# A transformer layer on eight cores: per-tile LayerNorm statistics and whole-tile query chains in place of pairs and halves

## The chip, the cores and the metric

The kernel runs on the 8 cores of one Trainium2 chip, the same program on each, every core on its own two sequences of 2048 tokens. The cores don't talk to each other. The metric is the device time of the slowest core in microseconds.

## What is computed

x is 16 x 2048 x 1024 in fp32. It is normalised once (LayerNorm without weights), and from the result two branches are computed and added to x: linear attention with 16 heads of 64, and a feed-forward part whose 8 binary trees of depth 7 mask the activations.

```python
xn = (x - mean) / sqrt(var + 1e-5)
q, k, v = (split_heads(xn @ W.T + b) for W, b in ((Wq,bq), (Wk,bk), (Wv,bv)))
q, k = feature_map(q), feature_map(k)          # where(x > 0, x + 1, exp(x))
kv = einsum('bhnd,bhnm->bhdm', k, v);  k_sum = k.sum(axis=2)
attn = (q @ kv / maximum(q . k_sum, 1e-6)) @ Wo.T + bo
logits = xn @ W_in.T + b_in                    # 8 trees x 255 nodes = 2040
acts = silu(logits);  dmap = nodes on the path that (logits > 0) takes, per tree
y = x + attn + (acts * dmap) @ W_out.T
```

## The kernel before

A core has 32 tiles of 128 tokens, 16 for each of its two sequences. Weights stay in SBUF as bf16. The code is written by hand, instruction by instruction, each engine with its own queue in program order; `em.wait` makes an engine wait for a semaphore value and `em.sig` raises one. Two loops run over the tiles, since the attention needs the sums over all tokens of a sequence first.

**Pass 1** (L336 on) computes K and V of a tile and adds to the sums `p_kv` and `p_ksb` of its sequence. TensorE's order in iteration t is: K matmuls of t (L344), the sums of tile t-1 (L309 to L319), the 8 transposes of the normalised tile t+1 (`emit_xnt`, L265), the V matmuls of t (L370, L378). K goes through ScalarE (copies at L352 and L356, the copy of the transposed tile at L271, Relu at L389, Exp at L392), V is copied by the vector engine (L396, L399), which also makes `s_phik` (L404). The LayerNorm statistics come in two parts: `emit_sums` takes the row sum on the vector engine (L200) and the sum of squares on ScalarE (L195), and `emit_pair` turns the sums of two tiles into mean and reciprocal root with 21 instructions on 128 x 2 numbers, each waiting for the one ahead (a reciprocal and four Newton steps). `emit_xnstt` (L253) then writes each normalised tile `s_xn`. Pairs are emitted at the end of even iterations, for tiles t+2 and t+3. There are four x buffers and two of `s_xn`. The statistics are kept in `s_stats` for pass 2.

**Pass 2** (L635 on) reloads x, normalises it with the stored statistics (`emit_ln`, L182), and computes query, trees and output. TensorE's order in iteration t is: Wq matmuls of t+1 (L462, L464), first half of the logits of t+1 (L479), the transposes of `s_qp` of t in two groups of four (L654, L659), the attention products in two groups of eight heads (L674, L683), the transposes of the masked activations (L698, L700), the Wo matmuls (L714, L716), the transposes of tile t+2 (L265), the W_out matmuls (L742), the second half of the logits of t+1. On the vector engine iteration t is: two calls of `emit_phiq_half` (L535 to L560, each six instructions, four of them on 512 columns), the final product of the mask (L601, L605), then for tile t+1 the comparisons (L502, L506), the activations (L513) and the mask levels (L574, six of L586), the two halves of the output sum (L750, L754), the normalisation of tile t+3 (L182) and the second half of the activations. ScalarE: copies of `s_qpt` (L664, L667) and of `s_ap` (L690, L693), of the transposed mask (L704 to L707), then tanh (L492), Relu and Exp (L519, L522) for tile t+1, the copy of the transposed tile (L271) and tanh again. On the SyncE queue the store of tile t stands ahead of the x load of tile t+3 (L174), and waits for the output sum of t. The two halves of the logits share one PSUM tile `p_L`.

Of the kernel before, what the change touches and what calls it, by code (L numbers as in the profile page):

```python
# [72 lines left out]
def build_nc():  # L73
# [103 lines left out]
    def emit_ln(t, ev_x):  # L177
        buf = t % 2
        xb = t % 4
        i_t = t % NT  # L180
        em.wait("V", ev_x, war_xn[buf])
        i = V.tensor_scalar(s_xn[buf], s_x[xb], s_stats[:, 2 * i_t:2 * i_t + 1],  # L182
                            s_stats[:, 2 * i_t + 1:2 * i_t + 2],
                            ALU.subtract, ALU.mult)
        ev = em.sig(i, "sv")
        war_x[xb] = ev
        return ev

    war_lnp = [None]

    def emit_sums(t, ev_x):
        p = t % 2
        xb = t % 4
        em.wait("S", ev_x, em.war.get(("sq",)), war_lnp[0])
        i = S.activation(s_phiq, s_x[xb], AF.Square,  # L195
                         accum_out=s_lnp[:, 2 + p:3 + p])
# [2 lines left out]
        em.wait("V", ev_x)
        i = V.reduce_sum(s_lnp[:, p:p + 1], s_x[xb], axis=AX.X)  # L200
        ev_sv = em.sig(i, "sv")
        return (ev_sv, ev_ss)

    def emit_pair(u, se0, se1):
        pstep = s_stats.ap[0][0]
        mean_ap = bass.AP(tensor=s_stats.tensor,
                          offset=s_stats.offset + 2 * u,
                          ap=[[pstep, 128], [2, 2]])
        rstd_ap = bass.AP(tensor=s_stats.tensor,
                          offset=s_stats.offset + 2 * u + 1,  # L210
                          ap=[[pstep, 128], [2, 2]])
        em.wait("V", se0[0], se0[1], se1[0], se1[1])
        i = V.tensor_scalar(mean_ap, s_lnp[:, 0:2], 1.0 / D, None, ALU.mult)
        e = em.sig(i, "sv")
        em.wait("V", e)
        i = V.tensor_tensor(s_lnp[:, 4:6], s_lnp[:, 0:2], mean_ap, ALU.mult)
        e = em.sig(i, "sv")
        em.wait("V", e)
        i = V.tensor_tensor(s_lnp[:, 6:8], s_lnp[:, 2:4], s_lnp[:, 4:6],
                            ALU.subtract)  # L220
        e = em.sig(i, "sv")
        war_lnp[0] = e
        em.wait("V", e)
        i = V.tensor_scalar(s_lnp[:, 8:10], s_lnp[:, 6:8], 1.0 / D, EPS_LN,
                            ALU.mult, ALU.add)
# [21 lines left out]
        return e

    def emit_xnstt(u, ev_y):
        xb = u % 4  # L250
        buf = u % 2
        em.wait("V", ev_y, war_xn[buf])
        i = V.tensor_scalar(s_xn[buf], s_x[xb],  # L253
                            s_stats[:, 2 * u:2 * u + 1],
                            s_stats[:, 2 * u + 1:2 * u + 2],
                            ALU.subtract, ALU.mult)
# [268 lines left out]
    def rn_ap_h(h5):  # L525
        return bass.AP(tensor=s_norm.tensor, offset=s_norm.offset + 16 + 8 * h5,
                       ap=[[s_norm.ap[0][0], 128], [1, 8], [0, HD]])

    def emit_phiq_half(t, h5, ev_e2_t, ev_qmm_t):
# [1 line left out]
        bb = t // TPB
        hc = 512 * h5
        if h5 == 0:
            em.wait("V", ev_e2_t, ev_qmm_t, war_scr.get("phiq"))
        i = V.scalar_tensor_tensor(s_phiq[:, hc:hc + 512], acc[:, hc:hc + 512],  # L535
                                   0.0, s_scr2[:, hc:hc + 512],
                                   ALU.max, ALU.add)
# [283 lines left out]
```

How the kernel before makes its waits and increments, by code:

```python
    def wait(self, e, *evs):  # L57
        for ev in evs:
            if ev is None:
                continue
            s, v = ev
            if v <= self.seen[e][s]:
                continue
            self.eng[e].wait_ge(self.sems[s], v)
            self.seen[e][s] = v
# [1 line left out]
    def sig(self, inst, s, k=1):  # L67
        self.cnt[s] += k
        inst.then_inc(self.sems[s], k)
        return (s, self.cnt[s])
```

## Time and profile before

| | |
|---|---|
| median of three runs | 1470.37 us (1469.67 to 1471.55) |
| the profiled execution | 1474.33 us, span 1473.3 us on the slowest core |
| spans of the 8 cores | 1464.2 to 1473.3 us |
| TensorE busy | 1259.3 us, 85% of the span |
| vector engine busy | 670.9 us, 46% |
| ScalarE busy | 463.6 us, 31% |
| chain that ended last | TensorE 53%, vector engine 25%, DMA 11% |
| granted TensorE clock, mean of the slowest core | 0.895 |

The chain that ended last is followed back from the last instruction, at each step to what released it. Busy shares are means over both passes, which have different limits. In the timeline a row merges neighbouring instructions of one line; the second number is the time from the first start to the last end, and the bracket tells how long the engine stood idle before and what released it. Matmuls overlap by a part of their latency, so their spacing is shorter than the duration of one.

### The profile page before, as it was taken

The page shows a single profiled execution, that of the slowest core. Times are in us where ns is not written, and L with a number is a line of the kernel's source. Part 1 is how long each engine was busy: PE and PEld are TensorE (multiplying, and loading weights), DVE is VectorE, ACT ScalarE, POOL GpSimd, SP SyncE. Part 2 cuts the span into 40 slices and gives each one's busy share as a digit, 9 for nine tenths or more (in the row PEclk, how much of TensorE's full clock was granted, in tenths as well). Part 3 has the DMA queues.
Part 4 walks back from the last instruction along what each step waited for, and adds up shares of the span by engine and source line. Part 5 has one row for each costly group of instructions (what it writes and reads, how often), then busy time and mean ns, then how long its engine had stood idle before and what let it go on. Part 6 is the DMA issues. An engine that isn't in the chain of part 4 may idle for free.

```text
span 1473.3 us, 18331 instructions; the slowest of 8 cores (1464.2 to 1473.3 us)
## 1 busy us (share of the span) xinstructions
PE 1259.3 (85%) x6784; PEld 564.1 (38%) x6784; DVE 670.9 (46%) x1399; ACT 463.6 (31%) x609; POOL 8.5 (1%) x15
## 2 busy tenths in 40 slices
PE   2787878878878898989999898998999989989896
PEld 0233333323333344444444444443444444444443
DVE  2344444454453354554445444454444544445443
ACT  1333333433433332234222342222422233222331
POOL 1000000000000000000000000000000000000000
PEclk9898998988988899998999889998999988999898
DMA  9971001101002511000010000100001000010000
GB/s 183 183 122 57 29 29 58 29 30 57 29 30 43 86 30 58 29 29 29 29 58 29 30 29 29 58 29 30 29 29 57 30 29 30 29 58 29 30 15 29
DMA packets 21607, 68.32 MB, mean 46 GB/s; under 512 B 2071, under 2 KB 2071, under 8 KB 21520
## 3 DMA queue, kind: packets, MB, share of 16 engines
q1 hardware_dynamic: 14112, 50.40, 10.5%
q0 software_dynamic: 7408, 16.76, 7.5%
q8 instruction: 55, 0.90, 0.3%
q14 instruction: 32, 0.26, 0.1%
HBM read 67.13 MB, written 16.78 MB: 57 GB/s over the span
## 4 chain that ended last, share of the span: by engine, by line
PE 53%; DVE 25%; DMA 11%; issue 7%; ACT 2%; DVEq 1%; SPq 1%; POOL 0%; ACTq 0%; POOLq 0%
PE p_acc L742 15%; DMA s_x<-x 9%; PE p_acc L714 5%; PE p_acc L716 5%; PE p_kq L370 4%; PE p_tr L698 4%; DVE s_scr L540 3%; PE p_kq L378 3%; DVE s_qp L560 3%; DVE s_norm L544 3%; DVE s_phiq L535 3%; DVE s_acts L513 3%; PE p_kq L344 3%; DMA s_wkv<-wvt 3%; PE p_v L370 2%
## 5 line engine op out<-in xcount | busy, mean ns | idle before, releaser
L479 PE MATMUL p_L<-s_win,s_xnt 128*128 128x510 bf16 x1024 | 235.3, 382 | 8.9 <-DVE s_acts L513 8.9
L742 PE MATMUL p_acc<-s_wkv,s_mT 128*128 128x512 bf16 (+1 forms) x1024 | 226.4, 379 | 0.0
L492 ACT ACTIVATE s_acts<-p_L 128x1020 bf16<-128x1020 f32 x64 | 66.4, 1037 | 313.4 <-PE p_L L484 313.4
L479 PEld LDWEIGHTS p_L<-s_win,s_xnt 128*128 128x128 bf16 x1024 | 97.6, 98 | 139.9 <-issue 27.7
L742 PEld LDWEIGHTS p_acc<-s_wkv,s_mT 128*128 128x128 bf16 (+1 forms) x1024 | 98.8, 98 | 114.0
L714 PE MATMUL p_acc<-s_wo,s_ap 128*128 128x512 bf16 x256 | 119.9, 468 | 0.0
L716 PE MATMUL p_acc<-s_wo,s_ap 128*128 128x512 bf16 x256 | 116.7, 456 | 0.0
L462 PE MATMUL p_acc<-s_wq,s_xnt 128*128 128x512 bf16 x256 | 99.8, 390 | 3.0 <-ACT s_xnt L271 3.0
L265 PE MATMUL p_xnt<-s_ident,s_xn 128*128 128x128 bf16 x256 | 25.9, 262 | 88.1 <-DVE s_xn L253 88.1
L464 PE MATMUL p_acc<-s_wq,s_xnt 128*128 128x512 bf16 x256 | 99.3, 388 | 0.0
L502 DVE TENSOR_SCALAR s_dn<-s_acts 128x1020 bf16<-128x1020 bf16 x32 | 13.7, 427 | 186.7 <-ACT s_acts L492 186.7
L664 ACT COPY s_qpt<-p_tr 128x512 bf16<-128x512 bf16 x32 | 18.8, 586 | 248.7 <-PE p_tr L654 248.7
L344 PE MATMUL p_kq<-s_wkv,s_xnt 128*128 128x512 bf16 x344 | 83.4, 386 | 10.9 <-DMA s_wkv<-wkt 10.9
L182 DVE TENSOR_SCALAR s_xn<-s_x,s_stats 128x1024 bf16<-128x1024 f32 x32 | 25.9, 812 | 145.7 <-DMA s_x<-x 145.7
L513 DVE SCALAR_TENSOR_TENSOR s_acts<-s_acts,p_L 128x1020 bf16<-128x1020 bf16 x64 | 77.4, 1210 | 16.0 <-ACT s_acts L492 16.0
L659 PE MATMUL p_tr<-s_ident,s_qp 128*128 128x128 bf16 x128 | 16.5, 272 | 71.5 <-DVE s_qp L560 71.5
L586 DVE TENSOR_TENSOR s_masked<-s_masked,s_dn 128x32 bf16<-128x32 bf16 (+2 forms) x192 | 64.0, 334 | 20.7 <-DVE s_masked L586 0.9
L271 ACT COPY s_xnt<-p_xnt 128x1024 bf16<-128x1024 bf16 x32 | 32.4, 1012 | 108.8 <-PE p_xnt L265 108.8
L754 DVE TENSOR_TENSOR s_out<-p_acc,s_x 128x512 f32<-128x512 f32 x32 | 22.1, 691 | 84.6 <-PE p_acc L742 84.6
L265 PEld LDWEIGHTS p_xnt<-s_ident,s_xn 128*128 128x128 bf16 x256 | 20.8, 117 | 98.8 <-issue 95.3
L396 DVE CAST s_v<-p_kq 128x512 bf16<-128x512 f32 x21 | 14.5, 692 | 93.8 <-PE p_kq L373 93.8
L370 PE MATMUL p_kq<-s_wkv,s_xnt 128*128 128x512 bf16 x168 | 57.0, 499 | 0.0
(115 smaller groups left out, 1648.6 us busy)
## 6 DMA issues: line engine op xcount, KB each, us to landing
s_x<-x SPq DMA_DIRECT2D x64, 512.0 KB, 4.3
y<-s_out SPq DMA_DIRECT2D x32, 512.0 KB, 2.9
s_win<-wint POOLq DMA_DIRECT2D x1, 4080.0 KB, 93.8
s_wkv<-woutt POOLq DMA_DIRECT2D x1, 3840.0 KB, 29.2
s_wkv<-wkt POOLq DMA_DIRECT2D x1, 2048.0 KB, 26.5
s_wkv<-wvt POOLq DMA_DIRECT2D x1, 2048.0 KB, 38.3
s_wq<-wqt POOLq DMA_DIRECT2D x1, 2048.0 KB, 49.5
s_wo<-wot POOLq DMA_DIRECT2D x1, 2048.0 KB, 64.8
```

Source lines behind the costliest of these rows:

```text
L344: T.matmul(bk, s_xnt[buf][:, 128 * c:128 * (c + 1)], s_wkv[:, 1024 * c + 512 * half:1024 * c + 512 * (half + 1)], start=(c == 0), stop=False)
L370: T.matmul(BNK[r2], s_xnt[buf][:, 128 * c:128 * (c + 1)], s_wkv[:, 8192 + 1024 * c:8192 + 1024 * c + 512], start=(c == 0), stop=False)
L462: T.matmul(acc[:, 0:512], lhs, s_wq[:, 1024 * c:1024 * c + 512], start=(c == 0), stop=False)
L464: T.matmul(acc[:, 512:1024], lhs, s_wq[:, 1024 * c + 512:1024 * (c + 1)], start=(c == 0), stop=False)
L479: T.matmul(p_L[:, 512 * k4:512 * k4 + 510], lhs, s_win[:, WIDTH * c + 510 * kk:WIDTH * c + 510 * (kk + 1)], start=(c == 0), stop=False)
L492: i = S.activation(s_acts[pb][:, 1020 * phase:1020 * (phase + 1)].rearrange("p (b c) -> p b c", b=2), srcL, AF.Tanh, scale=0.5)
L513: i = V.scalar_tensor_tensor(sl, sl, 1.0, srcL, ALU.add, ALU.mult)
L586: i = V.tensor_tensor(bass.AP(tensor=s_masked.tensor, offset=s_masked.offset + o2, ap=[[pstep, 128], [sdd, 2], [1, sdd]]), bass.AP(tensor= ...
L698: i = T.transpose(p_tr[:, 128 * jc:128 * (jc + 1)], s_masked[:, 128 * jc:128 * (jc + 1)], s_ident)
L714: T.matmul(acc[:, 0:512], lhs, s_wo[:, 1024 * c:1024 * c + 512], start=(c == 0), stop=False)
L716: i = T.matmul(acc[:, 512:1024], lhs, s_wo[:, 1024 * c + 512:1024 * (c + 1)], start=(c == 0), stop=False)
L742: i = T.matmul(acc[:, 512 * half:512 * (half + 1)], lhs, s_wkv[0:kj, 1024 * j + 512 * half: 1024 * j + 512 * (half + 1)], start=False, sto ...
```

## The change

In pass 1 `emit_sums`, `emit_pair` and `emit_xnstt` go. `emit_ln` computes the statistics of one tile with 20 instructions on 128 x 1 numbers, on its own scratch for each of two buffers, and normalises it; it is called at the end of iteration t for tile t+2, behind the load of that tile. In pass 2 the two half chains become one on 1024 columns, and so do the transposes of `s_qp`, the copies of `s_qpt` and `s_ap` and the attention products. The tanh of the first logits of t+1 is emitted at the top of the iteration, Relu and Exp of t+1 behind the query chain and ahead of the copy of `s_qpt` (both stood behind the Wo matmuls). The mask levels of tile t move from the iteration before into iteration t, behind the query chain. The second group of transposes of `s_qp` no longer uses the upper half of `p_tr`.

```diff
     def emit_ln(t, ev_x):
...
+        if t >= NT:
+            em.wait("V", ev_x, war_xn[buf])
+            i = V.tensor_scalar(s_xn[buf], s_x[xb], st_m, st_r,
+                                ALU.subtract, ALU.mult)
+            ev = em.sig(i, "sv")
+            war_x[xb] = ev
+            return ev
+        ln = s_ln[buf]
+        em.wait("S", ev_x, em.war.get(("sq",)), war_ln[buf])
+        i = S.activation(s_phiq, s_x[xb], AF.Square, accum_out=ln[:, 1:2])
...
+        i = V.reduce_sum(ln[:, 0:1], s_x[xb], axis=AX.X)
...
+        i = V.tensor_scalar(st_m, ln[:, 0:1], 1.0 / D, None, ALU.mult)
...
+        i = V.scalar_tensor_tensor(ln[:, 3:4], ln[:, 0:1], st_m, ln[:, 1:2],
+                                   ALU.mult, ALU.subtract)
...
+        i = V.tensor_scalar(ln[:, 4:5], ln[:, 3:4], -1.0 / D, EPS_LN,
                             ALU.mult, ALU.add)
...
+        i = V.reciprocal(ln[:, 6:7], ln[:, 4:5])
...
         for _it in range(4):
...
+        i = V.tensor_scalar(s_xn[buf], s_x[xb], st_m, st_r,
                             ALU.subtract, ALU.mult)
...
-        if t + 3 < NT:
-            sums_ev[t + 3] = emit_sums(t + 3, ev_xl[t + 3])
-            if t % 2 == 0:
-                ev_y = emit_pair(t + 2, sums_ev[t + 2], sums_ev[t + 3])
-                ev_stt[t + 2] = emit_xnstt(t + 2, ev_y)
-                ev_stt[t + 3] = emit_xnstt(t + 3, ev_y)
-
         if t + 1 < NT:
             ev_xnTe = ev_xnTe_next
-        if t + 4 < NT:
-            ev_xl[t + 4] = emit_xload(t + 4)
+            if t + 2 < NT:
+                ev_x2 = emit_xload(t + 2)
+                ln_next = emit_ln(t + 2, ev_x2)
...
+            nxt["_th1"] = emit_ffn_tanh(t + 1, nxt["_L1"], 0)
...
+        i = V.scalar_tensor_tensor(s_phiq, acc, 0.0, s_scr2, ALU.max, ALU.add)
...
+        i = V.tensor_tensor(s_scr1, s_phiq, s_ksb[b], ALU.mult)
...
+        i = V.reduce_sum(s_norm[:, 0:NH].rearrange("p (h o) -> p h o", o=1),
+                         s_scr1.rearrange("p (h d) -> p h d", h=NH), axis=AX.X)
...
+        i = V.tensor_scalar(s_norm[:, 16:32], s_norm[:, 0:NH], EPS_AT, None, ALU.max)
...
+        i = V.reciprocal(s_norm[:, 16:32], s_norm[:, 16:32])
...
+        i = V.tensor_tensor(s_qp.rearrange("p (h d) -> p h d", h=NH),
+                            s_phiq.rearrange("p (h d) -> p h d", h=NH),
+                            rn_ap, ALU.mult)
...
+        if t + 1 < NT:
+            nxt["ev_e2"] = emit_echain(t + 1, nxt["ev_qmm"])
...
+        em.wait("T", ev_qp, xnTe_next)
+        for c in range(8):
             i = T.transpose(p_tr[:, 128 * c:128 * (c + 1)],
                             s_qp[:, 128 * c:128 * (c + 1)], s_ident)
...
+        i = S.copy(s_qpt, p_tr[:, 0:1024])
...
+        for h in range(NH):
...
+        i = S.copy(s_ap, acc)
...
-            nxt["_th1"] = emit_ffn_tanh(t + 1, nxt["_L1"], 0)
-            nxt["ev_e2"] = emit_echain(t + 1, nxt["ev_qmm"])
-
-        if t + 1 < NT:
             av = emit_ffn_acts(t + 1, nxt["_th1"], 0)
+            nxt["dec_nd"] = av[1:]
...
-            nxt["mlev"] = emit_mask_levels(t + 1, av[1:])
```

## Rows read from the trace of the kernel before

**Rows 1.** Timeline of TensorE in pass 1: start us, us, engine, line, out<-in, count [idle before].

```profile
277.24 1.01 PE L265 MATMUL p_xnt<-s_ident,s_xn 128*128 128x128 bf16 x8 [4.62 <-DVE s_xn L253]
...
284.75 1.90 PE L344 MATMUL p_kq<-s_wkv,s_xnt 128*128 128x512 bf16 x8
...
289.87 0.61 PE L265 MATMUL p_xnt<-s_ident,s_xn 128*128 128x128 bf16 x8
```

**Rows 2.** Timeline of the vector engine in pass 1, same columns.

```profile
269.26 1.21 DVE L200 TENSOR_REDUCE s_lnp<-s_x 128x1 f32<-128x1024 f32 x1
270.64 0.17 DVE L213 TENSOR_SCALAR s_stats<-s_lnp 128x2 f32<-128x2 f32 x1 [0.17 <-DVE s_lnp L200]
...
276.28 1.53 DVE L253 TENSOR_SCALAR s_xn<-s_x,s_stats 128x1024 bf16<-128x1024 f32 x2
...
286.66 1.21 DVE L200 TENSOR_REDUCE s_lnp<-s_x 128x1 f32<-128x1024 f32 x1
```

**Rows 3.** Timeline of TensorE, first and last stalled transposes and the last tile.

```profile
59.35 1.01 PE L265 MATMUL p_xnt<-s_ident,s_xn 128*128 128x128 bf16 x8 [4.61 <-DVE s_xn L253]
...
440.97 1.01 PE L265 MATMUL p_xnt<-s_ident,s_xn 128*128 128x128 bf16 x8 [4.61 <-DVE s_xn L253]
...
453.65 0.61 PE L265 MATMUL p_xnt<-s_ident,s_xn 128*128 128x128 bf16 x8
...
458.39 0.82 PE L344 MATMUL p_kq<-s_wkv,s_xnt 128*128 128x512 bf16 x3
```

**Rows 4.** Timeline of TensorE in one tile of pass 2.

```profile
963.91 0.40 PE L654 MATMUL p_tr<-s_ident,s_qp 128*128 128x128 bf16 x4
966.50 0.59 PE L659 MATMUL p_tr<-s_ident,s_qp 128*128 128x128 bf16 x4 [2.19 <-DVE s_qp L560]
...
967.91 0.64 PE L683 MATMUL p_acc<-s_qpt,s_kvb 64*64 64x128 bf16 x8 [0.26 <-ACT s_qpt L667]
968.48 1.78 PE L698 MATMUL p_tr<-s_ident,s_masked 128*128 128x128 bf16 x15
...
970.16 0.63 PE L714 MATMUL p_acc<-s_wo,s_ap 128*128 128x512 bf16 x1
...
972.67 0.38 PE L714 MATMUL p_acc<-s_wo,s_ap 128*128 128x512 bf16 x1
```

**Rows 5.** Timeline of the vector engine around the same tile.

```profile
945.57 2.52 DVE L586 TENSOR_TENSOR s_masked<-s_masked,s_dn 128x32 bf16<-128x32 bf16 x6
...
957.29 0.81 DVE L182 TENSOR_SCALAR s_xn<-s_x,s_stats 128x1024 bf16<-128x1024 f32 x1 [4.69 <-DMA s_x<-x]
...
959.15 0.68 DVE L535 SCALAR_TENSOR_TENSOR s_phiq<-p_acc,s_scr 128x512 f32<-128x512 f32 x1
...
962.71 0.68 DVE L535 SCALAR_TENSOR_TENSOR s_phiq<-p_acc,s_scr 128x512 f32<-128x512 f32 x1
...
966.27 1.21 DVE L601 TENSOR_TENSOR s_masked<-s_acts,s_masked 128x2032 bf16<-128x2032 bf16 x1
```

**Rows 6.** Timeline of ScalarE in the same tile.

```profile
972.32 1.05 ACT L492 ACTIVATE s_acts<-p_L 128x1020 bf16<-128x1020 f32 x1
...
975.53 1.01 ACT L271 COPY s_xnt<-p_tr 128x1024 bf16<-128x1024 bf16 x1
```

**Rows 7.** Timeline of TensorE, Wo matmuls of a late tile, the next, and tile 29.

```profile
1032.89 0.63 PE L714 MATMUL p_acc<-s_wo,s_ap 128*128 128x512 bf16 x1
...
1034.12 0.38 PE L716 MATMUL p_acc<-s_wo,s_ap 128*128 128x512 bf16 x1
...
1061.82 0.63 PE L714 MATMUL p_acc<-s_wo,s_ap 128*128 128x512 bf16 x1
...
1400.14 0.63 PE L714 MATMUL p_acc<-s_wo,s_ap 128*128 128x512 bf16 x1
```

**Rows 8.** Timeline of TensorE in the first tile of pass 2.

```profile
508.01 0.40 PE L654 MATMUL p_tr<-s_ident,s_qp 128*128 128x128 bf16 x4
...
511.70 0.38 PE L714 MATMUL p_acc<-s_wo,s_ap 128*128 128x512 bf16 x1
```

More of the change, by code:

```diff
@@ L105, in build_nc @@
     s_xnt = [al(f"s_xnt{i}", [128, D], BF16).ap() for i in range(2)]
-    s_lnp = al("s_lnp", [128, 16], F32).ap()
+    s_ln = [al(f"s_ln{i}", [128, 8], F32).ap() for i in range(2)]
     s_stats = al("s_stats", [128, 2 * NT], F32).ap()
@@ L180, in emit_ln @@
         i_t = t % NT
[L181 to L196, printed above, removed]
+        st_m = s_stats[:, 2 * i_t:2 * i_t + 1]
@@ L198, in emit_sums @@
         em.war[("sq",)] = ev_ss
[L199 to L224, printed above, removed]
+        em.wait("V", ev_x, war_ln[buf])
@@ L247, in emit_pair @@
[L247 to L255, printed above, removed]
+            em.wait("V", ev5)
+            i = V.tensor_tensor(ln[:, 5:6], ln[:, 6:7], ln[:, 6:7], ALU.mult)
+            ev5 = em.sig(i, "sv")
+            em.wait("V", ev5)
+            i = V.tensor_tensor(ln[:, 5:6], ln[:, 5:6], ln[:, 4:5], ALU.mult)
@@ L523, in emit_echain @@
         return em.sig(i, "ss")
[L525 to L529, printed above, removed]
-        acc = p_acc[t % 2]
[L531 to L537, printed above, removed]
+    ev_x = emit_xload(NT + 0)
@@ new lines, in build_nc @@
+    xnTe_next, _ = emit_xnt(NT + 1, ln1, ev_xnTe0, p_tr)
+    ev_x3 = emit_xload(NT + 2)
+    ln_for_xnt = emit_ln(NT + 2, ev_x3)
+    cur = dict(ev_e2=ev_e2_0, ev_qmm=ev_qmm0, dec_nd=av1[1:],
+               silu=[av1[0], av2[0]])
+    war_trhi = None
+    for t in range(NT):
+        b = t // TPB
+        buf = t % 2
+        tok0 = t * 128
+        acc = p_acc[t % 2]
+        nxt = {}
+        if t + 1 < NT:
+            nxt["ev_qmm"] = emit_qmm(t + 1, xnTe_next)
+            nxt["_L1"] = emit_logits(t + 1, 0)
+            nxt["_th1"] = emit_ffn_tanh(t + 1, nxt["_L1"], 0)
+        em.wait("V", cur["ev_e2"], cur["ev_qmm"], war_scr.get("phiq"))
+        i = V.scalar_tensor_tensor(s_phiq, acc, 0.0, s_scr2, ALU.max, ALU.add)
@@ L564, in emit_phiq_half @@
         ev_qp = em.sig(i, "sv")
-        return ev_phiq, ev_qp
-    def emit_mask_levels(t, dec_nd):
-        pb = t % 2
-        dnb = s_dn[pb]
+        war_scr["phiq"] = ev_qp
+        if t + 1 < NT:
+            nxt["ev_e2"] = emit_echain(t + 1, nxt["ev_qmm"])
+        dec_nd = cur["dec_nd"]
+        dnb, actsb = s_dn[buf], s_acts[buf]
         pstep = s_masked.ap[0][0]
         dnstep = dnb.ap[0][0]
-        em.wait("V", *dec_nd)
-        em.wait("V", war_scr.get("masked"))
+        em.wait("V", *dec_nd, war_scr.get("masked"))
@@ L654, in build_nc @@
+        for c in range(8):
             i = T.transpose(p_tr[:, 128 * c:128 * (c + 1)],
                             s_qp[:, 128 * c:128 * (c + 1)], s_ident)
-        ev_qpT0 = em.sig(i, "st")
-        em.wait("T", ev_qp1, war_trhi)
-        for c in range(4, 8):
-            i = T.transpose(p_tr[:, 1024 + 128 * (c - 4):1024 + 128 * (c - 3)],
-                            s_qp[:, 128 * c:128 * (c + 1)], s_ident)
-        ev_qpT1 = em.sig(i, "st")
-        war_scr["qp"] = ev_qpT1
-        em.wait("S", ev_qpT0, war_scr.get("qpt"))
@@ L664, in build_nc @@
-        i = S.copy(s_qpt[:, 0:512], p_tr[:, 0:512])
-        ev_qpTe0 = em.sig(i, "ss")
-        em.wait("S", ev_qpT1)
-        i = S.copy(s_qpt[:, 512:1024], p_tr[:, 1024:1536])
-        ev_qpTe1 = em.sig(i, "ss")
-        em.wait("T", ev_qpTe0, kv_evac[b], ev_phiq0)
-        for h in range(0, 8):
+        ev_qpT = em.sig(i, "st")
+        war_scr["qp"] = ev_qpT
+        em.wait("S", ev_qpT, war_scr.get("qpt"))
+        i = S.copy(s_qpt, p_tr[:, 0:1024])
+        ev_qpTe = em.sig(i, "ss")
+        em.wait("T", ev_qpTe, kv_evac[b], ev_phiq)
@@ L677, in build_nc @@
                          start=True, stop=True, tile_position=(64 * a, 64 * a))
[L678 to L693 removed]
+        ev_apmm = em.sig(i, "st")
+        war_scr["qpt"] = ev_apmm
+        em.wait("S", ev_apmm, war_scr.get("ap"))
+        i = S.copy(s_ap, acc)
         ev_ape = em.sig(i, "ss")
[L696 removed]
+        em.wait("T", ev_mk, ev_qpTe, war_trhi)
         for jc in range(15):
@@ L708, in build_nc @@
         ev_mTe1 = em.sig(i, "ss")
+        war_trlo = ev_mTe0
         war_trhi = ev_mTe1
```

163 lines of the change are left out of this document (47 added, 116 removed).

## The prediction

> **What bounds the kernel now.** I read the page first: the chain of waits (shares by engine and line) says that no single engine is the bound; matrix work, the vector engine and one load take turns. So each of the two passes over the tiles has to be read as a loop of its own, from the timeline of each engine.
>
> *Pass 1 (key and value).* In the timeline of TensorE [rows 1] tile after tile runs 8 transposes, the V matmuls, the next tile's K matmuls and the sums over tokens. Every second tile the transposes of L265 wait: those at 277.24 stood idle for 4.62 us until L253 had written s_xn. Those at 289.87 did not, since both tiles of a pair get their normalised rows from one chain on the vector engine. That chain is in [rows 2]: the row sum at 269.26, 21 small instructions from 270.64 to 276.28 (5.64/21 = 0.269 us each), two normalisations. The pattern holds through the pass [rows 3]: stalled transposes at 59.35 and 440.97 with 14 pairs between them, 381.62/14 = 27.26 us a pair, 13.63 a tile. After a stall the matmuls are slow: transposes and V matmuls take 284.75 - 277.24 = 7.51 us behind a stall [rows 1] and 458.39 - 453.65 = 4.74 without one [rows 3]. This is TensorE at the lower of its two rates, 1.2 in place of 2.4 GHz, and worth 2.77 us.
>
> *Pass 2 (query, tree, output).* TensorE [rows 4] ends the logits at 963.91, transposes half of s_qp, waits 2.19 us for the other half, then does the attention products, the mask transposes (968.48) and from 970.16 the 16 Wo matmuls. The vector engine [rows 5] starts late because the x tile of L182 lands late; then two half chains from 959.15 and 962.71, then the masks at 966.27. The load in its turn waits for the output of the tile before. So the loop is output, store, load, normalise, s_phiq, s_qp, Wo, output. It takes (1400.14 - 970.16)/14 = 30.71 us a tile [rows 7].
>
> **The change, pass 1.** Each tile now has its own statistics chain, 20 small instructions in place of 21 for two tiles. It is emitted at the end of iteration t for tile t+2, and the transposes of t+2 come one iteration later, as far ahead as the first tile of a pair has today. So every tile becomes what every second one is now. Its loop: from the transposes to the row sum, 286.66 - 277.24 = 9.42 (V matmuls behind a stall, two copies, s_phik); from the row sum to the next transposes 277.24 - 269.26 = 7.98, less one small instruction, 7.71. Together **17.13 us a tile**. TensorE has its other work done 289.87 - 277.24 = 12.63 after the transposes [rows 1], so it idles 4.5 us, about what precedes the slow stretch today; I therefore keep the low rate in each tile. Bounds: if the rate never fell, 17.13 - 2.77 = 14.36; if it stayed low throughout, the 4.74 would double to 9.5, 2.0 more than the 7.51, 19.1.
>
> The small instructions shrink from 2 columns to 1. No row shows 1 column. Two columns take nearly all their time as a fixed part (0.269 each when each waits for the one ahead), so I keep 0.269, which is also the upper bound; the lower one is that the next one follows as soon as the 0.17 of the one ahead are over [rows 2]: 20 x 0.10 = 2.0 us less a tile, a loop of 15.1. The Trainium skill bears on this ("VectorE: DVE Perf Modes", the section on the fixed extra latency per instruction): it gives an fp32 instruction of N columns (N+151)/0.96 ns, which is 159 ns here, and its DRAIN section says that a semaphore between two of them costs nothing extra. By that the loop would be 20 x 0.11 = 2.2 us shorter, 14.9. The trace agrees with the duration (0.17) but not with the free semaphore: the spacing of dependent ones is 0.269 [rows 2].
>
> Tile 2's transposes come at 59.35 - 0.27 = 59.1. Twenty-nine tiles later, 59.1 + 29 x 17.13 = 555.9, come those of tile 31, at 453.65 now [rows 3]: +102.2. Behind a stall they and the V matmuls take 2.77 more: **+105**. Moved with it: the x loads are issued two tiles ahead in the code, not four, but the SyncE queue waits only for a buffer freed by the normalisation four tiles back, so they still run ahead. Square stays behind the Exp on ScalarE, where it is now, and every chain still follows it. The load of the output weights (GpSimd queue) waits for the last V matmul and shifts with everything. The evacuation of the sums after tile 15 fits in a stall, nothing.
>
> **The change, pass 2.** Vector engine: the halves of a tile become whole. One half chain is 3.56 us [rows 5], of which four wide instructions 4 x 0.69 = 2.76 and 0.80 for two small ones and the hand-offs. A wide instruction on 1024 columns takes 1.21 (the row sum of [rows 2]). So 4 x 1.21 + 0.80 = 5.64 in place of 7.12: s_qp is whole at 959.15 + 5.64 = 964.8, 1.5 us earlier than its second half now, 0.9 later than TensorE could have begun. The mask levels, now done in idle time before the output (2.52 for six [rows 5], and one small one), come behind it with the final product (1.21) and another small one: 964.8 + 2.52 + 0.27 + 1.31 + 0.27 = 969.2.
>
> ScalarE: tanh, Relu and Exp of the next tile now come before the copy of s_qpt. Tanh needs the logits, which end at 963.91; the three take 975.53 - 972.32 = 3.21 [rows 6]. A hand-off between engines costs about 0.15 (the first normalisation, 276.28 + 0.81, to the transposes at 277.24). So the copy starts at 963.91 + 0.15 + 3.21 = 967.3 although its transposes were done by 965.9, and takes 1.01 [rows 6] to 968.3. TensorE idles there 2 to 3 us. Then 16 attention products (968.48 - 967.91 = 0.57 for eight [rows 4], so 1.14) from 968.4 to 969.6, with the masks ready at 969.2, and mask transposes as now, 1.68, to 971.2. Wo starts there, not at 970.16: **about 1.0 us later a tile**. Bounds of this term: 0.7 if the next instruction on ScalarE starts 0.1 before the one ahead ends each time, 1.6 if a wide instruction that reads PSUM costs the vector engine 0.1 to 0.2 more than 1.21. What lay on DVE's path is no longer late; what is late next is ScalarE.
>
> Then the rate. Wo begins at the low rate, 0.63 a matmul, and the first at 0.38 is at 972.67 [rows 4], 2.51 us in; run at the full rate that stretch would be half, so 1.25 us of each tile is lost there. One tile came late [rows 7]: Wo at 1032.89, which is 62.73 behind 970.16 where two mean intervals make 61.42. It had the full rate after 1.23 us, and the next Wo came only 28.93 later. So a late tile does not push the return of the rate back with it, and gets its delay back. If that holds when every tile is 1.0 longer, the delay adds up over a few tiles until the low stretch in Wo is 2.0 us shorter; from there each tile wins its 1.0 back and the mean interval is near 30.7 again. I take this as the likelier case, with 0.05 a tile left over: 29 x 0.05 = 1.5. If it does not hold, the tile pays 1.0, and the restart being later costs one or two more low matmuls (0.2 each): +1.4 a tile, 41.
>
> Tile 0 has no slow Wo now: 3.69 us from logits to Wo [rows 8]. It gets 0.15 + 3.21 + 1.01 + 0.15 + 1.14 + 1.68 = 7.34, +3.7, and up to 1.25 for the rate; with what the next tiles give back or lose until they settle I estimate +4. The last two tiles have no load in the loop and less to give back, 1.0 each: +2. Pass 2: 1.5 + 4 + 2 = **+7.5**, against +47 in the other case.
>
> **The sum.** The profiled execution took 1474.3 us (span 1473.3); 1474.3 + 105 + 7.5 = 1586.8. It lies 4.0 over the median of 1470.4, so **1583 us**.
>
> **Rivals.**
> - *Pass 2 gives nothing back*: 105 + 47 = 152, 1622 us; with half given back about 1603. For it: the low stretch starts at a restart, and TensorE now restarts only at 968.4. Against: the late tile.
> - *Small instructions follow each other without a gap*: the loop of pass 1 is 15.1, 29 x 2.0 = 58 us less: 1525. The same rival covers a rate that stays high in pass 1: 29 x 2.77 = 80 less, 1503. Against both: 14 stalls that all look alike. The page on VectorE named above would give 29 x 2.2 = 64 less, 1519.
> - *Pass 1 stays low for longer*: up to 29 x 2.0 = 58 more, 1641; half of it, 1612, is nearer, since today's stalls of 4.6 us show no sign of it.
> - *Faster*: a one-column instruction that hardly waits for the one ahead. With spacing s pass 1 changes by 29 x 20 x (0.269 - s); it outweighs the 112.5 from s = 0.075 down, and at 0.05 the kernel takes 1456. Its place is the statistics chain alone. Against: two-column ones last 0.16 to 0.17 by themselves [rows 2].
> - *The change does nothing*, because the chain is hidden: TensorE already waits 4.6 us for half the tiles with half as many chains, so there is nothing left to hide it behind.
>
> **Chances and range.** Forecast (1572 to 1592) 0.58; pass 2 gives back half or less (1592 to 1625) 0.21; cheaper pass 1 (1480 to 1572) 0.10; low for longer, 0.09; faster 0.02. The range takes the first two and the nearer half of the low-rate case: 1572 to 1625. This measurement tells about 0.2% from no change. Slower by over 0.2% 0.97, within 0.01, faster 0.02.
>
> **What would show it.** Pass 1: transposes of L265 stalled in front of every tile by about 4.5 us, intervals of 17.1; at 14 to 15 the small instructions or the rate were misjudged. Pass 2: the copy of s_qpt directly behind Exp, TensorE idle before the attention products, Wo about 7.3 behind the logits, intervals near 30.7 with only one or two low Wo matmuls. Intervals of 31.5 or more with as many low ones as now would refute the give-back. I would be wrong altogether if the transposes of pass 1 did not wait in each tile.

## The result and the profile after

The changed kernel takes 1615.29 us in the median, against 1471.78 us for the kernel before: ratio **1.0975**, 95% interval 1.0962 to 1.0988. It is slower, as forecast and inside the range, but 32 us above the 1583 of the forecast and next to the 1622 of the first rival. The profiled execution has a span of 1615.9 us, 142.6 more than before.

The page of the changed kernel, engines and chain that ended last:

```profile
PE 1274.4 (79%) x6688; PEld 573.9 (36%) x6784; DVE 695.7 (43%) x1511; ACT 454.8 (28%) x545; POOL 8.5 (1%) x15
...
PE 45%; DVE 31%; DMA 11%; issue 10%; ACT 1%; DVEq 1%; SPq 1%; POOL 0%; ACTq 0%; POOLq 0%
```

TensorE is busy for nearly as long as before, in a longer span; the share of the chain that the vector engine holds went from 25% to 31%. The mean granted clock of the slowest core went from 0.895 to 0.870.

Timeline of TensorE in pass 1, for [rows 1, 3] (L238 are the transposes of the next tile, L308 the K matmuls):

```profile
58.85 1.01 PE L238 MATMUL p_xnt<-s_ident,s_xn 128*128 128x128 bf16 x8 [4.31 <-DVE s_xn L228]
...
263.19 1.01 PE L238 MATMUL p_xnt<-s_ident,s_xn 128*128 128x128 bf16 x8 [4.30 <-DVE s_xn L228]
...
270.57 1.90 PE L308 MATMUL p_v<-s_wkv,s_xnt 128*128 128x512 bf16 x8
...
280.15 1.01 PE L238 MATMUL p_xnt<-s_ident,s_xn 128*128 128x128 bf16 x8 [4.30 <-DVE s_xn L228]
...
553.29 1.01 PE L238 MATMUL p_xnt<-s_ident,s_xn 128*128 128x128 bf16 x8 [4.43 <-DVE s_xn L228]
...
560.69 1.90 PE L308 MATMUL p_kq<-s_wkv,s_xnt 128*128 128x512 bf16 x8
```

Every tile waits now, for 4.3 us. From tile 2 to tile 31 there are 29 intervals in 494.44 us, **17.05** each; the worked-out one was 17.13. The V matmuls behind a stall take 7.38 to 7.40 us, as the 7.51 of [rows 1].

Timeline of the vector engine in the same stretch, for [rows 2]:

```profile
272.49 1.21 DVE L196 TENSOR_REDUCE s_ln<-s_x 128x1 f32<-128x1024 f32 x1
273.81 0.15 DVE L199 TENSOR_SCALAR s_stats<-s_ln 128x1 f32<-128x1 f32 x1
...
278.92 0.16 DVE L224 TENSOR_TENSOR s_stats<-s_ln 128x1 f32<-128x1 f32 x1
279.19 0.81 DVE L228 TENSOR_SCALAR s_xn<-s_x,s_stats 128x1024 bf16<-128x1024 f32 x1
```

The 20 small instructions start at 273.81 and give way to the normalisation at 279.19: 5.38/20 = 0.269 us each, with one column as with two.

Timeline of TensorE in one tile of pass 2, for [rows 4, 7]: L442 end the logits, L584 transpose s_qp, L596 are the attention products, L608 and L610 the mask transposes, L625 and L627 Wo.

```profile
1280.49 0.60 PE L442 MATMUL p_L<-s_binr,s_allone 1*128 1x510 bf16 x2
1282.19 0.61 PE L584 MATMUL p_tr<-s_ident,s_qp 128*128 128x128 bf16 x8 [1.10 <-DVE s_masked L550]
1285.32 0.63 PE L596 MATMUL p_acc<-s_qpt,s_kvb 64*64 64x128 bf16 x16 [2.52 <-ACT s_qpt L589]
1286.49 1.76 PE L608 MATMUL p_tr<-s_ident,s_masked 128*128 128x128 bf16 x15 [0.54 <-DVE s_masked L576]
1288.04 0.31 PE L610 MATMUL p_tr<-s_ident,s_masked 128*120 128x128 bf16 x1
...
1289.42 0.38 PE L627 MATMUL p_acc<-s_wo,s_ap 128*128 128x512 bf16 x1
```

The first wait is for s_qp: the code waits for L536, and the profile names the short instruction behind it. From the end of the logits (1280.49 + 0.53) to Wo at 1288.15 it is 7.13 us, where [rows 4] have 6.25. A record of the first Wo matmul is missing in each tile, so Wo is taken to start 0.11 behind the last mask transpose, as in the tiles of before. ScalarE and the vector engine at the same time, for [rows 5, 6]:

```profile
1281.19 1.02 ACT L450 ACTIVATE s_acts<-p_L 128x1020 bf16<-128x1020 f32 x1 [7.11 <-PE p_L L442]
...
1284.18 0.99 ACT L589 COPY s_qpt<-p_tr 128x1024 bf16<-128x1024 bf16 x1
```

```profile
1276.21 1.22 DVE L518 SCALAR_TENSOR_TENSOR s_phiq<-p_acc,s_scr 128x1024 f32<-128x1024 f32 x1
...
1280.82 1.23 DVE L536 TENSOR_TENSOR s_qp<-s_phiq,s_norm 128x1024 bf16<-128x1024 f32 x1
1281.96 0.17 DVE L550 TENSOR_SCALAR s_masked<-s_dn 128x16 bf16<-128x16 bf16 x1
1282.23 2.52 DVE L562 TENSOR_TENSOR s_masked<-s_masked,s_dn 128x32 bf16<-128x32 bf16 x6
1284.85 1.22 DVE L572 TENSOR_TENSOR s_masked<-s_acts,s_masked 128x2032 bf16<-128x2032 bf16 x1
1286.17 0.17 DVE L576 TENSOR_SCALAR s_masked<-s_acts 128x8 bf16<-128x8 bf16 x1
```

The copy of s_qpt (L589) waits behind tanh, Relu and Exp and starts 2.99 us after tanh. The masks are ready at 1286.34 and the mask transposes follow at 1286.49; the attention products were done half a microsecond earlier. So the last wait in front of Wo is the mask work on the vector engine, by a little.

To see where the time of pass 2 went I cut each tile into three parts: Wo (to the transposes of the next tile), from there to the end of the logits (W_out, logits, Wq, logits), and from there to the next Wo. Means over 28 or 29 tiles on the slowest core of each profiled kernel, without the first and the last ones, in us:

| kernel | Wo | W_out to end of logits | logits to Wo | interval |
|---|---|---|---|---|
| before | 4.62 | 19.79 | 6.24 | 30.65 |
| changed | 4.42 | 19.99 | 7.33 | 31.75 |

The second part takes 19.64 when nothing waits in it, and Wo 3.4 at the full rate, by the best tiles of the runs below. The cores of one execution differ: the mean interval of before is 30.40 to 30.67 over the eight, that of the changed kernel 31.44 to 31.78, so a difference of 0.2 between two rows of this table says little by itself.

### The profile page after: what moved, and what is told of

The parts are those of the page before. It is cut to its first block, busy times and chain, and to the rows that moved or that the text cites. A ratio compares the mean times of both kernels' runs of the same rounds, so it can differ in the third digit from the quotient of the medians.

```text
span 1615.9 us, 18281 instructions; the slowest of 8 cores (1600.4 to 1615.9 us)
## 1 busy us (share of the span) xinstructions
PE 1274.4 (79%) x6688; PEld 573.9 (36%) x6784; DVE 695.7 (43%) x1511; ACT 454.8 (28%) x545; POOL 8.5 (1%) x15
## 4 chain that ended last, share of the span: by engine, by line
PE 45%; DVE 31%; DMA 11%; issue 10%; ACT 1%; DVEq 1%; SPq 1%; POOL 0%; ACTq 0%; POOLq 0%
PE p_acc L649 14%; DMA s_x<-x 8%; PE p_acc L627 5%; PE p_kq L334 4%; PE p_acc L625 4%; PE p_tr L608 3%; DVE s_masked L562 3%; PE p_kq L342 3%; DMA s_wkv<-wvt 2%; PE p_v L334 2%; DVE s_phik L368 2%; DVE s_acts L471 2%; DVE s_scr L522 2%; DVE s_norm L526 2%; DVE s_qp L536 2%
## 5 line engine op out<-in xcount | busy, mean ns | idle before, releaser
L238 PE MATMUL p_xnt<-s_ident,s_xn 128*128 128x128 bf16 x256 | 32.0, 303 | 149.4 <-DVE s_xn L228 149.4
L657 DVE TENSOR_TENSOR s_out<-p_acc,s_x 128x512 f32<-128x512 f32 x32 | 22.1, 691 | 277.9 <-PE p_acc L649 277.9
L627 PE MATMUL p_acc<-s_wo,s_ap 128*128 128x512 bf16 x256 | 114.5, 447 | 6.9 <-issue 6.9
L422 PE MATMUL p_acc<-s_wq,s_xnt 128*128 128x512 bf16 x256 | 98.2, 384 | 2.0 <-ACT s_xnt L244 1.8
L420 PE MATMUL p_acc<-s_wq,s_xnt 128*128 128x512 bf16 x254 | 97.6, 384 | 1.4 <-ACT s_xnt L244 1.4
L625 PE MATMUL p_acc<-s_wo,s_ap 128*128 128x512 bf16 x224 | 98.4, 439 | 0.0
L308 PE MATMUL p_kq<-s_wkv,s_xnt 128*128 128x512 bf16 x344 | 83.6, 387 | 10.8 <-DMA s_wkv<-wkt 10.8
L596 PE MATMUL p_acc<-s_qpt,s_kvb 64*64 64x128 bf16 x512 | 28.9, 274 | 78.2 <-ACT s_qpt L589 78.2
L244 ACT COPY s_xnt<-p_xnt 128x1024 bf16<-128x1024 bf16 x32 | 32.4, 1012 | 179.6 <-PE p_xnt L238 179.6
L238 PEld LDWEIGHTS p_xnt<-s_ident,s_xn 128*128 128x128 bf16 x256 | 24.4, 136 | 163.3 <-issue 163.3
L334 PE MATMUL p_kq<-s_wkv,s_xnt 128*128 128x512 bf16 x167 | 74.0, 620 | 0.2 <-issue 0.2
L608 PE MATMUL p_tr<-s_ident,s_masked 128*128 128x128 bf16 x480 | 56.1, 308 | 14.6 <-DVE s_masked L576 14.2
L661 DVE TENSOR_TENSOR s_out<-p_acc,s_x 128x512 f32<-128x512 f32 x32 | 22.1, 692 | 86.5 <-PE p_acc L649 86.5
```

Of the source, the lines that this page charges most:

```text
L308: T.matmul(bk, s_xnt[buf][:, 128 * c:128 * (c + 1)], s_wkv[:, 1024 * c + 512 * half:1024 * c + 512 * (half + 1)], start=(c == 0), stop=False)
L334: T.matmul(BNK[r2], s_xnt[buf][:, 128 * c:128 * (c + 1)], s_wkv[:, 8192 + 1024 * c:8192 + 1024 * c + 512], start=(c == 0), stop=False)
L420: T.matmul(acc[:, 0:512], lhs, s_wq[:, 1024 * c:1024 * c + 512], start=(c == 0), stop=False)
L422: T.matmul(acc[:, 512:1024], lhs, s_wq[:, 1024 * c + 512:1024 * (c + 1)], start=(c == 0), stop=False)
L608: i = T.transpose(p_tr[:, 128 * jc:128 * (jc + 1)], s_masked[:, 128 * jc:128 * (jc + 1)], s_ident)
L625: T.matmul(acc[:, 0:512], lhs, s_wo[:, 1024 * c:1024 * c + 512], start=(c == 0), stop=False)
```

## The experiments

Ratios are to runs of the kernel before on the same chip. Where pass 2 of a kernel is meant, the parts of its mean tile are in the table at the end of this section.

### The two passes by themselves

e1_pass1 takes only the hunks of pass 1 (`emit_ln`, its calls), e2_pass2 only those of pass 2.

> Pass 1 as changed, pass 2 as before. My reading of the changed kernel's trace (29 intervals of 17.05 us in pass 1 in place of 13.6, plus 2.7 for the last V matmuls): +102 us, ratio 1.069. Rival, that the slower pass 1 also disturbs pass 2 (later weight loads, other state of the TensorE rate at its start): +110 or more.

> Pass 2 as changed, pass 1 as before. If each tile pays the 1.15 us that Wo comes later and little is given back: 31 x 1.15 to 1.3 = +36 to +41 us, ratio 1.025 to 1.028. If the give-back of the prediction held with pass 1 untouched: +7 us, ratio 1.005.

Measured: pass 1 alone 1581.3 us, ratio 1.0728 (1.0707 to 1.0750), +107; pass 2 alone 1513.5 us, ratio 1.0269 (1.0254 to 1.0285), +39. Together 0.0997 against the 0.0975 of the whole change, so the passes add. Pass 1 lies between its two expectations. On the mean, pass 2 pays what Wo comes later (1.10 us a tile in the table above), so the give-back that the prediction counted on does not show in the total.

### Four Newton steps made two

```diff
-        for _it in range(4):
+        for _it in range(2):
...
-            i = V.tensor_tensor(st_r if _it == 3 else ln[:, 6:7],
+            i = V.tensor_tensor(st_r if _it == 1 else ln[:, 6:7],
```

> The changed kernel with two Newton steps in place of four in each statistics chain of pass 1 (part of the computation is left out): 8 of 20 small instructions fewer. If the chain of small instructions sets the loop of pass 1, each tile is at least 8 x 0.269 = 2.15 us shorter: 29 x 2.15 = 62 us less than the changed kernel, ratio 1.055 to before; more (to 90 us less) if the shorter idle time also keeps TensorE's rate up. Rival, that another wait is right behind it: under 30 us less.

Measured: 1520.5 us, ratio 1.0338 (1.0290 to 1.0386), 95 less than the changed kernel. The transposes come every 13.73 us on average instead of 17.05 and stall for 2.2 instead of 4.3. The chain sets the loop; 3.3 us a tile went for 2.15 us of instructions, and 95 us is a little more than the 90 that I had as the most. The rest is TensorE's rate, by the rows: behind a stall the transposes and V matmuls take 240.26 - 234.09 = 6.17 us here and 7.38 in the changed kernel, 1.2 less, and 2.15 + 1.2 is the 3.3.

```profile
234.09 1.01 PE L238 MATMUL p_xnt<-s_ident,s_xn 128*128 128x128 bf16 x8 [2.20 <-DVE s_xn L228]
...
240.26 1.90 PE L308 MATMUL p_kq<-s_wkv,s_xnt 128*128 128x512 bf16 x8
```

### Which part of pass 2 costs

e3_merge_alone is pass 2 as changed, with tanh, Relu and Exp behind Wo and the mask levels in the iteration before, as they were. e5_echain_late moves back only the first, e6_levels_early only the second. The moves, in short:

```diff
+            nxt["_th1"] = emit_ffn_tanh(t + 1, nxt["_L1"], 0)
+            nxt["ev_e2"] = emit_echain(t + 1, nxt["ev_qmm"])
+
             av = emit_ffn_acts(t + 1, nxt["_th1"], 0)
...
+            nxt["mlev"] = emit_mask_levels(t + 1, av[1:])
```

> Only the halves become whole; tanh, Relu and Exp stand behind Wo again, the mask levels in the iteration before (pass 1 as before). Theory that ScalarE's and the masks' new places cost the time and not the merging: Wo starts about 6.0 us behind the logits, not 7.3, and the kernel takes -5 to +3 us against before. Rival, that losing the overlap of the two halves is what costs: at least half of the cost of pass 2 is still there, +18 us or more.

> Pass 2 as changed (pass 1 as before), but tanh, Relu and Exp behind Wo again; the mask levels stay behind the query chain. Theory of two tied waits (ScalarE at 968.4, masks at 969.2 in the prediction's working): the attention products start about 2 us earlier, but the mask transposes still wait for the masks, so Wo moves by under 0.5 us and the kernel stays at +25 to +39 us. Rival, that ScalarE's order alone is the cost: +0 us or less.

> Pass 2 as changed (pass 1 as before), but the mask levels in the iteration before again; tanh, Relu and Exp stay ahead of the copy of s_qpt. Theory of two tied waits: ScalarE still holds the attention products, Wo moves by under 0.3 us, +30 to +39 us. Rival, that the mask levels alone are the cost: +0 us or less.

Measured: e3 1452.7 us, ratio 0.9854 (0.9822 to 0.9886), 22 us **less** than before; e5 1515.1, ratio 1.0264 (1.0215 to 1.0314), as much as with both in their new places; e6 1486.4, ratio 1.0070 (1.0042 to 1.0099). So whole query chains are a gain, larger than I expected (its intervals are of two kinds, 27.8 to 28.9 and 29.9 to 31.8; the mean of 29.75 is that of no tile); moving ScalarE's work back alone brings nothing; moving the mask levels back alone brings 29 us, more than I expected. Both together bring 61. Seen from e3, each move costs by itself, ScalarE's 32 us (e6) and the mask levels' 60 (e5), and the two don't add, since each has its own wait. TensorE in a tile of e5, where the mask transposes (L646) wait for the masks, and in one of e6, where the products (L643) wait for ScalarE's copy and the mask transposes (L655) for nothing:

```profile
1018.45 0.63 PE L634 MATMUL p_acc<-s_qpt,s_kvb 64*64 64x128 bf16 x16 [1.25 <-ACT s_qpt L627]
1020.90 1.76 PE L646 MATMUL p_tr<-s_ident,s_masked 128*128 128x128 bf16 x15 [1.82 <-DVE s_masked L614]
```

```profile
1102.13 0.64 PE L643 MATMUL p_acc<-s_qpt,s_kvb 64*64 64x128 bf16 x16 [2.45 <-ACT s_qpt L636]
1102.69 1.62 PE L655 MATMUL p_tr<-s_ident,s_masked 128*128 128x128 bf16 x15
```

### A pure delay

The kernel before with memsets on a buffer that nothing else uses, ahead of `emit_phiq_half`: one of 512 columns (e7), or one of 1024 and one of 256 (e9, shown):

```diff
+        for (o, w) in ((0, 1024), (1024, 256)):
+            V.memset(s_dum[:, o:o + w], 0.0)
         ev_phiq0, ev_qp0 = emit_phiq_half(t, 0, cur["ev_e2"], cur["ev_qmm"])
```

> The kernel before with one extra memset (512 columns, on a tile of its own) on the vector engine ahead of the query chain, a delay of some 0.4 to 0.6 us a tile. If a late tile gets its delay back from the rate, as the prediction assumed: under 5 us in all. If nothing comes back: 31 x 0.4 to 0.6 = 12 to 19 us.

> The kernel before with memsets of 1024 and of 256 columns ahead of the query chain, together some 1.15 us a tile, the delay that the change brings, with nothing else changed. The small delay (0.40 us a tile) had cost 7 us in all. If that share holds (0.6 paid): 31 x 1.15 x 0.6 = 21 us. If what the change showed holds (Wo 1.09 later, 1.10 a tile paid): 31 to 39 us. If the prediction's full give-back holds: under 5 us.

Measured: e7, with 0.40 us from the start of the memset to that of s_phiq, 1482.7 us, ratio 1.0049 (1.0025 to 1.0073), 8 us in place of 12; e9, with 1.10 us, 1500.2 us, ratio 1.0186 (1.0167 to 1.0204), 27 in place of 34. Something comes back in both, and far from all: 0.6 of the small delay is paid in the whole kernel and 0.8 of the one of a microsecond. Tile by tile e9 says where. In tiles 8 to 11 of its slowest core Wo starts at 768.73, 799.38, 830.16 and 860.90, intervals of 30.6 to 30.8 as before, with Wo itself at 3.8 us: there all of the 1.10 comes back. It is paid in the first four intervals (32.9, 32.4, 31.3 and 32.4, where before has 30.3, 30.4, 29.0 and 31.7) and at each late x load: the interval into the late tile is 32.1, 32.4 and 32.2 (before 31.2, 32.0 and 31.4), and the next one still 32.0, 32.2 and 31.6, where before is back at 30.6, 28.9 and 30.3.

### The load ahead of the store

In e10_after_load_first (the changed kernel) and e13_load_first (the kernel before) the x load of tile t+3 stands ahead of the store of tile t on the SyncE queue. Its buffer was freed one tile earlier.

```diff
+        if t + 3 < NT:
+            ev_x2 = emit_xload(NT + t + 3)
         em.wait("Y", ev_fin)
         i = Y.dma_start(out=y_d[tok0:tok0 + 128, :], in_=s_out[buf])
         ev_prev_out[buf] = em.sig(i, f"so{buf}", 16)
 
         if t + 3 < NT:
-            ev_x2 = emit_xload(NT + t + 3)
```

> The changed kernel with the x load of tile t+3 on the SyncE queue ahead of the store of tile t in pass 2. If late loads are what keeps the tiles from settling near 30.8 us: the vector engine starts 1 us earlier, the logits never wait, intervals settle, -20 to -30 us against the changed kernel (ratio to before 1.077 to 1.084). Rival, that the path then goes over ScalarE (tanh behind the logits): little, -5 to -10 us (1.09 to 1.094), Wo still about 7.3 behind the logits.

> The kernel before with the x load of tile t+3 ahead of the store of tile t in pass 2, nothing else. The combined kernel took 196 us off, where early statistics (95) and whole chains (22) make 117: 79 are left for the load. If that is the load's own part: ratio about 0.947. If it is the sum of small stalls that lets TensorE's rate fall, and only all of them removed keep it up (whole chains and early load together): the load alone brings 10 to 35 us, ratio 0.976 to 0.993.

Measured: e10 1583.5 us, ratio 1.0750 (1.0731 to 1.0769), 32 less than the changed kernel; its logits no longer wait, its mean interval is 30.74, but single ones don't settle: every second or third is 31.2 to 31.4, the others 30.3 to 30.5. e13 1374.3 us, ratio **0.9293** (0.9214 to 0.9372), 100 less than before, where I had expected 10 to 35. The timelines of TensorE in e10 and in e13, a tile each:

```profile
1038.66 0.60 PE L442 MATMUL p_L<-s_binr,s_allone 1*128 1x510 bf16 x2
1039.46 0.61 PE L584 MATMUL p_tr<-s_ident,s_qp 128*128 128x128 bf16 x8 [0.20 <-DVE s_masked L550]
1043.49 0.63 PE L596 MATMUL p_acc<-s_qpt,s_kvb 64*64 64x128 bf16 x16 [3.42 <-ACT s_qpt L589]
```

```profile
1026.62 0.60 PE L484 MATMUL p_L<-s_binr,s_allone 1*128 1x510 bf16 x2
1027.16 0.40 PE L654 MATMUL p_tr<-s_ident,s_qp 128*128 128x128 bf16 x4
1029.11 0.38 PE L659 MATMUL p_tr<-s_ident,s_qp 128*128 128x128 bf16 x4 [1.55 <-DVE s_qp L560]
1029.42 0.41 PE L674 MATMUL p_acc<-s_qpt,s_kvb 64*64 64x128 bf16 x8
1030.32 0.41 PE L683 MATMUL p_acc<-s_qpt,s_kvb 64*64 64x128 bf16 x8 [0.48 <-ACT s_qpt L667]
1030.66 1.01 PE L698 MATMUL p_tr<-s_ident,s_masked 128*128 128x128 bf16 x15
```

In e13 the wait for the second half of s_qp is 1.55 us in this tile and about 1.2 in most, where [rows 4] have 2.19, and the 15 mask transposes behind it take 1.01 us, not 1.78: in most tiles TensorE keeps its full rate throughout, and Wo takes 3.42 on the mean. The vector engine's 1.0 us is thus the smaller part of the 3.35 that the mean interval lost; the rest came with the rate. In e10 it stands for 3.42 us in front of the attention products, whose x tiles come just as early, because the copy of s_qpt is behind tanh, Relu and Exp; there Wo begins low in every tile. So with the load out of the way the change costs more, not less: e10 takes 209 us more than e13, about 103 of them up to the first Wo of pass 2 and 105 behind it, where the same change of pass 2 cost 39 us with the late load (e2).

### Statistics one iteration earlier, and all together

e11_early_stats is the kernel before with sums of tile t+4, the pair of t+3 and t+4 (odd t) and the normalisation of t+3 at the end of iteration t; what stands ahead of the loop is moved to match (not printed). e12_combined has this, the whole query chains of e3 and the early load of e13.

```diff
+        if t + 4 < NT:
+            ev_xl[t + 4] = emit_xload(t + 4)
+            sums_ev[t + 4] = emit_sums(t + 4, ev_xl[t + 4])
+            if t % 2 == 1:
+                ev_y = emit_pair(t + 3, sums_ev[t + 3], sums_ev[t + 4])
         if t + 3 < NT:
-            sums_ev[t + 3] = emit_sums(t + 3, ev_xl[t + 3])
...
+            ev_stt[t + 3] = emit_xnstt(t + 3, ev_y)
```

> The kernel before with the statistics of pass 1 one iteration earlier (sums of tile t+4 and normalisation of tile t+3 at the end of iteration t), still in pairs. If the chain behind the transposes is the whole stall of pass 1 and the low rate its consequence: no tile waits, 14 x (4.62 + 2.77) = 103 us less, and what TensorE alone takes is 9.85 us a tile in place of 13.63; ratio 0.93. Rival, that the vector engine is the next bound (6 to 8 us of work a tile, 12 with the chain): less than half of it, 0.965 or more.

> The earlier statistics, whole query chains with tanh, Relu, Exp and the mask levels in their old places, and the x load ahead of the store. If the parts add: -103, -22, and 20 to 31 for a load that no longer waits: 1320 to 1335 us, ratio 0.90. Rival, that without stalls the kernel runs into TensorE's own work or a lower granted rate: 0.92 or more.

Measured: e11 1377.9 us, ratio 0.9357 (0.9342 to 0.9371); no transposes of pass 1 wait for s_xn, tiles take 9.85 and 10.48 us by turns. e12 1277.5 us, ratio **0.8675** (0.8662 to 0.8689), faster than both kernels and over 40 us under the lower end of what I expected, because the load by itself is worth 100 us (e13) and not 20 to 31; the parts by themselves make 95, 22 and 100, the whole 196. Its mean clock is 0.976, its usual interval in pass 2 27.04. Timeline of TensorE in e12:

```profile
1012.10 0.63 PE L639 MATMUL p_acc<-s_qpt,s_kvb 64*64 64x128 bf16 x16 [1.25 <-ACT s_qpt L632]
1012.67 1.01 PE L651 MATMUL p_tr<-s_ident,s_masked 128*128 128x128 bf16 x15
...
1013.98 0.38 PE L668 MATMUL p_acc<-s_wo,s_ap 128*128 128x512 bf16 x1 [0.25 <-ACT s_ap L646]
...
1036.54 0.60 PE L484 MATMUL p_L<-s_binr,s_allone 1*128 1x510 bf16 x2
1037.28 0.61 PE L627 MATMUL p_tr<-s_ident,s_qp 128*128 128x128 bf16 x8
1039.14 0.64 PE L639 MATMUL p_acc<-s_qpt,s_kvb 64*64 64x128 bf16 x16 [1.25 <-ACT s_qpt L632]
```

The mask transposes follow the products without a wait and at the full rate; what holds Wo last is the copy of s_ap (L646), by 0.25 us.

### Pass 2, tile by tile, of all of them

| kernel | Wo | W_out to end of logits | logits to Wo | interval |
|---|---|---|---|---|
| e1 pass 1 alone | 4.37 | 20.37 | 6.05 | 30.79 |
| e2 pass 2 alone | 4.46 | 20.05 | 7.36 | 31.86 |
| e3 whole chains alone | 4.43 | 19.82 | 5.51 | 29.75 |
| e5 masks late | 4.51 | 20.06 | 7.30 | 31.87 |
| e6 ScalarE's work early | 4.27 | 19.98 | 6.64 | 30.89 |
| e7 delay 0.40 | 4.15 | 20.06 | 6.60 | 30.81 |
| e9 delay 1.10 | 3.98 | 19.77 | 7.46 | 31.21 |
| e10 changed, load first | 4.56 | 19.64 | 6.54 | 30.74 |
| e11 early statistics | 4.31 | 20.26 | 6.11 | 30.68 |
| e12 combined | 3.81 | 19.63 | 3.90 | 27.34 |
| e13 load first | 3.42 | 19.64 | 4.24 | 27.30 |

## Why the prediction was right, and by how much it missed

**Pass 1, 17.13 us a tile: right.** 17.05 measured, the loop as described: every tile stalls, small instructions at 0.269 with one column as with two, the low rate behind each stall. K of tile 31 starts 102.3 us later (458.39 and 560.69), forecast +105; e1 shows +107 by itself. The Newton steps (e4) show the chain as the cause. The free semaphore that the Trainium skill gives ("VectorE: DVE Perf Modes", the section on the DRAIN) did not show: spacing 0.269, duration 0.15 to 0.17. The page measured it on a row of copies and its duration formula on 512 columns and more, not on instructions this small.

**Pass 2, whole halves: right in direction.** 5.64 us for a whole chain; from 1276.21 to 1281.96, the next instruction, it is 5.75. Masks ready 10.05 after the start of the chain forecast, 1286.34 - 1276.21 = 10.13 measured. e3 shows that the merging alone gains 22 us, which the text had only as 1.5 us less on the vector engine.

**Pass 2, Wo 1.0 us later: right, in part by luck.** 7.34 behind the logits was forecast, 7.33 is the mean (6.24 before, +1.09). I had ScalarE ahead by 0.4 us as what is late next; it is the mask work by half a microsecond, since the copy of s_qpt started 2.99 and not 3.21 behind tanh, and the sixteen products took 0.63 in one go, not 1.14. By the forecast's own times the masks alone give 969.2 + 0.15 + 1.68, 7.1 behind the logits, which is the tile shown (7.13); the mean has 0.2 more, from tiles after a late load or a jump of the rate. e5 and e6 show both waits, one close behind the other.

**The give-back: the step that failed.** "If that holds when every tile is 1.0 longer, ... from there each tile wins its 1.0 back and the mean interval is near 30.7 again." The means say -0.20 in Wo, and +0.20 by logits that wait for a late x load, so nothing on balance: 1.10 a tile in place of 0.05. Wo of tile 0 came 103.0 later (pass 1 and tile 0 as forecast within 6 us), and the 31 intervals after it took 39.7 us more, forecast about 4. The 36 us too few there, less the 6 that pass 1 and tile 0 were overestimated by, are the 30 by which the profiled execution (1616.96) lies above its forecast of 1586.8.

The late tile of [rows 7] was also read too simply. The 28.93 behind it are 1.8 under the mean interval. Its low stretch in Wo was 0.6 us shorter than the mean; the larger part, 1.0, came in front of the next Wo, where TensorE still had the full rate in the products and the first mask transposes (1.22 us for fifteen, against 1.78 in [rows 4]):

```profile
1060.70 1.22 PE L698 MATMUL p_tr<-s_ident,s_masked 128*128 128x128 bf16 x15
```

Why the give-back failed can be read from the row of intervals of the changed kernel. After a disturbance they do shrink as the argument said: Wo starts at 1194.43, 1225.99, 1257.21, 1288.15 and 1319.00, intervals 31.56, 31.22, 30.94, 30.85, while the part of Wo falls from 4.84 to 4.01. There it ends: at most 0.6 is left above the 3.4 of the full rate, and the next late load, or a tile whose low stretch is suddenly longer, puts the loop out of step. Timelines of TensorE in two neighbouring tiles:

```profile
1350.28 0.63 PE L627 MATMUL p_acc<-s_wo,s_ap 128*128 128x512 bf16 x1 [0.22 <-issue]
1350.70 0.45 PE L625 MATMUL p_acc<-s_wo,s_ap 128*128 128x512 bf16 x1
1350.99 0.38 PE L627 MATMUL p_acc<-s_wo,s_ap 128*128 128x512 bf16 x1
...
1381.28 0.63 PE L627 MATMUL p_acc<-s_wo,s_ap 128*128 128x512 bf16 x1 [0.22 <-issue]
...
1384.69 0.52 PE L627 MATMUL p_acc<-s_wo,s_ap 128*128 128x512 bf16 x1
1385.05 0.38 PE L625 MATMUL p_acc<-s_wo,s_ap 128*128 128x512 bf16 x1
```

With the record that is missing at the front, Wo has three low matmuls in the first tile and ten in the next, 31.0 later, and the interval behind that is 32.3. The one late tile of [rows 7] showed give-back from a state with 2.5 us of low stretch in hand; a change that uses up most of it in every tile keeps little for the disturbances, and each costs over a microsecond. e9 shows this by itself: its undisturbed tiles give the whole 1.10 back, and the first tiles and those around a late load pay. It is not all, though. e9 holds the vector engine up by as much as the change moves Wo, and costs 27 us where pass 2 of the change (e2) costs 39; its Wo is 0.64 shorter than before on the mean, that of the changed kernel 0.20. The other 12 us come with more late loads (logits wait in 10 tiles of e2 and in 5 of e9, on the slowest cores) and with jumps as in the second tile above, in which no load is late. The granted clock is 0.50 from 1347.4 and 0.99 again from 1350.8 in the first tile; in the second it is 0.50 from 1378.2 and back only from 1384.9, though it fell at nearly the same place, 4.8 and 4.7 us behind the logits. What makes the low stretch last twice as long there I have not isolated. That TensorE's idle time lies elsewhere in the tile (in the changed kernel in front of the transposes, the products and the masks, in e9 mostly in front of the second transposes) is a candidate, not shown.

**The rivals.** "Pass 2 gives nothing back" (0.21) is what happened on the mean. Cheaper small instructions, a pass 1 that stays low and the faster case are refuted by 17.05 and 0.269.

## What to carry to other kernels

Follow the chain of a loop past the wait that is seen: a wait of 4 us cost 7 here, since TensorE came back at half its rate, and a load that held the vector engine for 1.0 us a tile (2.30 from the end of the logits to the second L513 before, 1.30 in e13) was worth 100 us of 1474. Don't book such a loss as a reserve that will swallow a delay: here it gave the delay back in undisturbed tiles (e9), and once it was used up each late load or jump of the rate cost over a microsecond. When two moves lengthen two waits of one path, try each with the other taken back: here ScalarE's move looked free (e5 against e2) as long as the masks held Wo, and costs 32 us without them (e6 against e3).
